# A wait on POOL in the middle of each unit of gathers

## What is computed

```python
qh = (q_tok @ Wq.T + bq).reshape(-1, H, 2, HALF)
sub_scores = jnp.einsum('nhcf,hcef->nhce', qh, keys)
s, idx = jax.lax.top_k(sub_scores, K)
# the 8 best of 64 pairs for each of 8 heads
indices = jnp.take_along_axis(all_idx, best_pos, axis=-1)
w_down = w_down_embed[indices]
w_up = w_up_embed[indices]
x = jax.nn.gelu(jnp.einsum('nd,nhkd->nhk', q_tok, w_down))
vals = x * jax.nn.softmax(best_s, axis=-1)
out = jnp.einsum('nhk,nhkd->nd', vals, w_up)
```

## Time and profile before

| what | value |
|---|---|
| median of 3 runs, us | 3447.02 |
| lowest and highest run, us | 3434.35, 3462.33 |
| span of the profiled execution, us | 5577.0 |
| time given of the profiled execution beside its span | none |
| instructions | 53095 |
| busy, us: PE, DVE, ACT, POOL | 3254.3, 2619.7, 2226.7, 2330.6 |
| gathers, and the bytes of their queue | 2432, 316.15 MB |
| bytes of all DMAs | 519.04 MB |
| mean granted TensorE clock | 0.719 |

### The profile page before, as it was taken

The page is one execution under the profiler, slowest core; times in us unless marked ns, Lnnn a source line. Parts: engine busy times, 40 slices in busy tenths (PEclk is TensorE's granted clock), DMA queues, the critical chain, the costliest instruction groups (busy, mean ns, idle before and its releaser), DMA issues. The chain is left out here.

```text
span 5577.0 us, 53095 instructions
## 1 busy us (share of the span) xinstructions
PE 3254.3 (58%) x14195; PEld 2193.0 (39%) x14195; DVE 2619.7 (47%) x13857; ACT 2226.7 (40%) x4627; POOL 2330.6 (42%) x2451
## 2 busy tenths in 40 slices
PE   4356445556665554655655665656546655665678
PEld 2133233334334333443433434434333433443456
DVE  3443554544454445444543554554435445544633
ACT  2235232234543442344425433543534344344444
POOL 4544444353443444434344434443353444444410
PEclk7556677676777776787767777777767777776879
DMA  5223224142332432243233324333332333343320
GB/s 172 89 80 105 69 81 136 55 118 78 99 95 71 121 91 81 78 120 102 77 101 96 93 76 116 91 90 104 105 90 68 102 97 99 90 116 91 95 79 3
DMA packets 314967, 519.04 MB, mean 93 GB/s; under 512 B 56746, under 2 KB 171308, under 8 KB 314668
## 3 DMA queue, kind: packets, MB, share of 16 engines
q0 software_dynamic: 119808, 316.15, 20.5%
q10 hardware_dynamic: 86784, 130.06, 7.5%
q1 hardware_dynamic: 108076, 69.45, 4.2%
HBM read 498.64 MB, written 11.17 MB: 91 GB/s over the span
## 5 line engine op out<-in xcount | busy, mean ns | idle before, releaser
L766 POOL DMA_INDIRECT ring<-in_table_dram,idx x2432 | 2328.4, 957 | 3015.7 <-PE bank_u L861 1521.4
L1023 PE MATMUL bank_x<-z3t,w_b 128*128 128x255 f32 (+1 forms) x1264 | 425.7, 470 | 410.9 <-ACT eo L3302 194.0
L5409 DVE CUSTOM_DVE_ANT_0 ring<-ring,bank_q 128x128 f32<-128x128 f32 (+1 forms) x2432 | 537.4, 281 | 232.6 <-issue 176.4
L861 PE MATMUL bank_u<-ring,ident 128*128 128x512 f32 (+1 forms) x912 | 543.6, 743 | 151.7 <-ACT ring L3196 66.8
L3196 ACT ACTIVATE ring<-ring,vu 128x128 f32<-128x128 f32 (+1 forms) x1824 | 555.5, 390 | 131.5 <-DVE vu L5415 73.6
L3297 ACT ACTIVATE ht<-bank_x,b_s 128x255 f32<-128x255 f32 (+1 forms) x704 | 289.3, 463 | 657.6 <-remote 404.3
L1026 PE MATMUL bank_x<-ht,w_b 128*128 128x255 f32 (+1 forms) x1264 | 386.7, 459 | 207.5 <-ACT ht L3297 179.3
L1023 PEld LDWEIGHTS bank_x<-z3t,w_b 128*128 128x128 f32 x1264 | 269.4, 236 | 518.0 <-ACT eo L3302 211.8
L1026 PEld LDWEIGHTS bank_x<-ht,w_b 128*128 128x128 f32 x1264 | 283.6, 239 | 295.4 <-ACT ht L3297 197.9
L861 PEld LDWEIGHTS bank_u<-ring,ident 128*128 128x128 f32 (+1 forms) x912 | 206.3, 239 | 392.8 <-issue 280.6
L1070 PE MATMUL bank_x<-qd,tb 128*128 128x128 f32 x1280 | 227.1, 332 | 210.1 <-ACT gs L3227 100.9
(11 more groups left out here) (235 smaller groups left out, 5418.1 us busy)
## 6 DMA issues: line engine op xcount, KB each, us to landing
w_b<-in_w_dram ACTq DMA_DIRECT2D x304, 256.0 KB
ring<-in_table_dram,idx POOLq DMA_INDIRECT x2432
tb<-turned ACTq DMA_DIRECT2D x120, 256.0 KB
tb<-in_table_dram SPq DMA_DIRECT2D x120, 256.0 KB
tb<-turned SPq DMA_DIRECT2D x40, 256.0 KB
tb<-in_table_dram ACTq DMA_DIRECT2D x40, 256.0 KB
gs<-in_table_dram SPq DMA_DIRECT2D x32, 256.0 KB
turned<-gs ACTq DMA_DIRECT2D x32, 256.0 KB
```

The source lines that it names most:

```text
L766: pool.indirect_dma_start(ring[0:rows, u, k, :], None, table, bass.IndirectOffsetOnAxis(ap=idx[0:rows, j, c:c + 1], axis=0)).then_inc(gath ...
L861: ins = mm(U[0:rows, :], ident[0:rows, 0:rows], ring[0:rows, u, 4 * c:4 * c + 4, D:ROW], start=(u == 0 and c == 0), stop=(u == UNITS - 1 a ...
L1023: ins = mm(to[:, m * n:m * n + n], wa[:, k * D:(k + 1) * D], x, start=True, stop=True)
L5409: ins = dve.tensor_tensor_reduce(w, w, qrep[r, b, :], 1.0, 0.0, ALU.mult, ALU.add, xu[r, k:k + 1])
```

## The change

Ahead of the ninth gather of each unit (k = 8), POOL waits until `gathered[u]` has reached the value that it has when the first eight gathers of this unit have landed: 256 for each earlier tile, and 16 for each of the eight.

```diff
--- before.py
+++ after.py
@@ -763,6 +763,8 @@
                     pool.sem_inc(carried)
                     for k in range(UR):
                         c = u * UR + k
+                        if k == UR // 2:
+                            pool.wait_ge(gathered[u], (t * UR + k) * 16)
                         pool.indirect_dma_start(
                             ring[0:rows, u, k, :], None, table,
                             bass.IndirectOffsetOnAxis(ap=idx[0:rows, j, c:c + 1], axis=0)).then_inc(gathered[u], 16)
```

## The result

| | before | changed |
|---|---|---|
| median, us | 3447.05 (4 runs) | 3696.69 (4 runs) |
| lowest and highest, us | 3434.35, 3462.33 | 3683.91, 3702.53 |
| ratio to before, 95% interval | | 1.0715 [1.0678, 1.0752] |
| span of the recorded execution, us | 5577.0 | 3699.2 |

The change costs 250 us, 7.2%; the forecast was 297. The page of the changed kernel answers to the earlier trace rows: the span, the busy time of each engine, and the group of gathers.

The account below looks back on a forecast made before the run. The prediction took POOL's stream of gathers to bound the kernel. To the 3447 us median it added 312 for the waits and 8 for tile 0, less 23 filled: 3744 us, range 3560 to 3840.

Parts of the forecast that it names:

- What bounds the kernel: On POOL: without recording its stream of gathers is the bound; the trace's waits and standstills belong mostly to the recording.
- 0 to 93 us of waits: On POOL in the timed runs: the idle time left for indices or ring quarters, in place of the trace's 2021 us.
- Its sum: POOL's own time before the change: 58 + 90 + 2960 + 16 + 230 = 3354 us, against the 3447 median.
- Price of a wait: At each unit's ninth gather: a step of 3.3 us in place of 1.25, so 2.05 us each, 312 us for 152.
- The landing: From the eighth gather's start until its rows are in: taken as 2.5 us.
- The restart: POOL starting again from rest after the rows land: 0.8 us, from a gather that waited for a PE sum.
- What is filled: POOL's waits for indices or ring quarters shrink: half of an assumed 46 us, so 23 us off.
- the 8 us for tile 0: In tile 0's four units: 8 us added for dearer waits in a loaded queue, 16 us at most.
- Room on POOL: Rival, 9%: the unrecorded gather cadence is 1.17 us or less, the wait is hidden, time stays at 3447 within 1%.
- The pause lets the others through: Rival, 5%: pauses on POOL give PE, ACT and DVE a way in, a fifth of 333 us back; 3380 us.
- The fuller queues: Rival, 12%: rows land 0.6 us later in the timed runs' denser traffic, waits cost 403 us; 3835 us.
- What would show it: Changed trace: about 2.3 us idle before each ninth gather, 152 times, POOL busy 2328 us; span may hardly move or shorten.

Follow-up runs that it names:

- the second recording: The unchanged kernel before, recorded once more on another chip; its run took 3452.6 us and its recorded span is 3450.7 us.
- the run with fifteen gathers: Kernel before with 15 gathers per unit in place of 16, the sixteenth row's work reading the fifteenth's row; 3442.9 us, ratio 0.9979.
- the slow recording: The first recorded execution of the unchanged kernel before, which the prediction read; span 5577.0 us, against a median of 3447.05 us.
- the boundary kernel with the count: Kernel before with a wait for the previous unit's sixteenth gather, ahead of the count on `carried` before each unit's first gather; 3816.5 us, ratio 1.1034.
- fifteen gathers and the wait: Kernel before with 15 gathers per unit in place of 16 and the change's wait ahead of the ninth; 3550.2 us, ratio 1.0252.

## Why the prediction came out

**What bounds the kernel.** Half right. That the 2021 us of POOL's waits in the earlier trace rows and the standstills in the earlier trace rows are not in the timed runs was right, and the second recording shows it: 99 us of waits, 62 of them under their own labels. Its reason, that recording causes them, was too general; it was that one execution. "POOL's stream of gathers is the bound" holds for added work, but the run with fifteen gathers shows a second bound within 0.3% of it. The estimate of 0 to 93 us of waits was near the 99, in part by luck. Its sum took the 230 us behind the last gather from the slow recording; the second has 183.3 us there, and with it the sum is 3307 us and the room for waits 140. Against that, the mean step within a unit is 1.28 us, not 1.25, which is some 60 us over the 2280 steps within units.

**Price of a wait.** 2.05 us forecast, 2.36 measured. The landing was mis-sized: 2.5 us from the end of one train in the slow recording, 2.98 us as a mean over the changed kernel, where the DMA share between first and last gather is 0.50 in place of 0.33. The forecast named this and left it to a rival. The restart was 0.64 us for 0.8; the row used was a wait for PE that sits on the count on `carried`, and no run shows what that wait costs on the gather itself. By the page's estimate of 2.30 us for the landing (the Trainium skill, "DMA: Bandwidth & Descriptors", section "Anatomy of one DMA — SWDGE (gpsimd) path") the error of this term would have been larger. The total by it, 3713 us, would have been nearer to the 3696.7 measured, but only because the filled part was mis-sized the other way.

**What is filled.** 23 us forecast, 97 measured, the term with the largest error. The guess that a late consumer undoes half of it was wrong: half of the waits already filled everything. The two errors, 152 x 0.31 = 47 us up and 74 us down, with the 8 us for tile 0 (which the mean of 2.36 already holds) and 12 us of small terms (the shorter tail, 8 us, among them), bring 297 to 250. That the total came within 47 us is partly luck: the price was too low and the filled part too low, and these two pull against each other.

**The rivals.** Room on POOL: the cadence was the true one; the mean step in the unit is 1.27 to 1.30 us in the second recording, and most steps are 1.25. The pause lets the others through: there was nothing to let through. The fuller queues were real in their cause (2.98 us), but the fill was larger too.

**What would show it.** About 2.3 us ahead of the ninth gather, put down to a DMA, 152 times, was right (2.66 us, 149 times). The recorded span fell by 1878 us. The forecast had allowed for a shorter one because waits for PE would take up the new wait; the reason was that the first recording was out of line.

## What to carry to other kernels

A wait for landed data on the engine that issues it costs the flight time that has not passed yet plus a restart, for each wait; in this kernel, with the wait for rows asked four gathers earlier it costs nothing that can be measured, one gather earlier 66 us in place of 250. Before a stream is called the bound, take work from it as well as adding some: here 358 us added cost 250, and 190 us taken away gave 9. A long idle time that the view labels issue can be a wait: 41 us of the 99 here were. And where a recorded span is far from the timed runs, record again before reading its waits.

## What the runs showed of the hardware that was not expected

- A gather on POOL starts 0.64 us after the rows landed when it waits itself, and 1.17 to 1.20 us when a counting instruction takes up the wait. 152 times, that was 75 us in the middle of the unit.
- One recorded execution was 1.6 times as long as the timed runs, with ACT standing 41.92 us in the earlier trace rows, while POOL's cadence of 1.25 us in it was undisturbed.
- A gather lands 2.98 us after its start at a DMA share of 0.50 and 2.62 us at 0.33 (means over the eighth gathers of the units, in the changed kernel and in the first recording of before). With waits after every 4 gathers it is 2.8 to 2.9 us. That the share is the cause was not tried by itself.
- Some kernels have a pause of POOL once in five units, of 1.2 us each (29 times in the boundary kernel with the count), or as a ninth gather that starts 1.6 to 1.9 us after the landing (29 times with fifteen gathers and the wait). The cause isn't known.
